# Edge convolution on a graph: Fori loops written out, index loads and key preparation batched by 13 chunks

## The chip, the cores and the metric

One core of one Trainium2 chip runs the kernel. The time is that of the device in microseconds for one launch. The kernel before was run three times: median 5047.05 us, lowest 5042.66, highest 5049.33. One further execution was taken with the hardware profiler; its rows are what this document reads.

## The reference

The graph has 12,500 nodes with 64 features and 400,000 edges, sorted by destination. Cut to what matters:

```python
h = relu(layernorm(x))
x_i, x_j = h[dst], h[src]
feat = concat([x_i, x_j - x_i], -1)                 # 128 values per edge
m = relu(feat @ W1 + b1) @ W2 + b2                  # 64 values per edge
out = segment_max(m, dst, num_segments=12500)       # 0 where a node has no edge
return x + where(isneginf(out), 0, out)
```

The first product splits in two tables of one row per node: a row a that belongs to the destination and a row b that belongs to the source. Per edge only relu(a[dst] + b[src]) @ W2 and a running maximum over the edges of one destination are left.

## The kernel before, in words

The 400,000 edges lie in 128 lanes of 3125 consecutive edges. A tile is one edge of every lane (128 x 64 values), a chunk is 12 tiles, and there are 260 chunks and a tail of 5 tiles. `rows` is a ring of 26 chunks. The prologue makes both tables, stores them to HBM, scatters the a rows to the places of the first edges of each node (`a_edges`) and turns the whole b table into bf16 pages in SBUF (`shared`). Then five engines run the chunks side by side, each with its own program order, held together by semaphores only. What each does for chunk c:

- POOL (GpSimd) waits until PE has turned chunk c-26, whose ring slot it takes (`z_turned`), and for the source indices (`src_loaded`), adds one to `chunk_open`, and gathers 11 tiles of b rows by 11 indirect DMAs (`gather_chunk`, L393; the loop is L432 to L439).
- The 12th tile is not gathered but picked on PE out of the bf16 pages. Its source index is split into an octet number and a place in the octet by two DVE instructions (`split_src`, L920 and L921, chunk c+5), converted to floats by ACT (L537), spread as a diagonal by ACT (`spread_keys`, L540), turned by PE (`turn_keys`, L666), compared with the page keys by DVE (`match_keys`, L935, chunk c+4), multiplied with the pages by PE (`pick`, L676, 37 matmuls for chunk c+3, 21 before the messages and 16 after them), masked by ACT (L549, chunk c+2), where `mark_octets` (L927) gave the mask, and summed by DVE (`choose`, L944).
- SP loads the a rows of the chunk into one of two halves of `a_fill` (`load_a`, L334, when `a_free` allows it) and, per chunk, the 12 columns of source indices for the chunk 26 ahead (L343).
- ACT scales the flags of a chunk (`flags`, L530 and L531, three chunks ahead), takes the relu of the turned sums (L560), and starts the store of the finished maxima (L567).
- DVE adds a and b rows (`add`, L897, chunk c+1), carries a rows along the lane where an edge does not start a node (`fill`, L885, chunk c+2, twelve dependent steps) and takes the running maximum (`maximum`, L911, chunk c, twelve dependent steps); fills and maxima alternate.
- PE turns the sums of the chunk (L687, 6 transposes), picks the first half for chunk c+3, makes the messages with W2 (L696, 12 matmuls), turns the keys of chunk c+5 and picks the second half.

The order on each engine is written by hand. SP, POOL, ACT, PE and DVE each have a `Fori` over 10 (or 9) iterations with 26 chunks unrolled in it, so semaphore targets and DMA addresses that depend on the iteration are computed in registers. At the loop's end three extra picks and five extra key turns are done for chunks that do not exist, with credits given on semaphores so that every iteration has the same counts.

After the last chunk a small epilogue carries maxima across lanes, gathers the maximum of every node (L456) and adds x.

Of the kernel before, what the change touches and what calls it, by code (L numbers as in the profile page):

```python
# [15 lines left out]
P = 128  # L16


def edge_conv(nc, x, src, dst, W1, b1, W2, b2, out):
# [25 lines left out]
    KEEP = RING // 2  # L45
# [16 lines left out]
    FILL_AHEAD = 3  # L62
    PAGES_FIRST = PAGES // 2 + 1

    with ExitStack() as ctx:
# [20 lines left out]
        src_idx = sb("src_idx", [P, RING, CHUNK], I32)  # L86
        same = sb("same", [P, TILES + (FILL_AHEAD + 1) * CHUNK])
        keep = sb("keep", [P, KEEP, 2, CHUNK])
# [60 lines left out]
        key_bits = sb("key_bits", [P, 2, 2], I32)  # L149
        key_octet = sb("key_octet", [P, 2, 2])  # L150
# [60 lines left out]
        src_first = sem("src_first")  # L211
        chunk_open = sem("chunk_open")
        src_loaded = [sem(f"src_loaded{s}") for s in range(RING // 2)]
        gathered = [sem(f"gathered{s}") for s in range(RING)]
        a_loaded = [sem(f"a_loaded{s}") for s in range(AE_RING)]
        a_free = sem("a_free")
# [29 lines left out]
        bits_split = sem("bits_split")  # L246
        bits_converted = sem("bits_converted")
# [28 lines left out]
        def _(sp):  # L276
            sp.dma_start(dst_rows[0:NP, :], dst.rearrange("(p k) -> p k", p=NP)).then_inc(samples_loaded, 16)
            for q in range(PIECES):
                sp.dma_start(xs[0:NP, q * PJ:(q + 1) * PJ, :],
                             x_nodes[:, q * PJ:(q + 1) * PJ, :]).then_inc(x_loaded[q], 16)  # L280
            sp.dma_start(src_idx[:, :, :].rearrange("p r k -> p (r k)"),
                         src_lanes[:, 0:RING * CHUNK]).then_inc(src_first, 16)
# [40 lines left out]
            for k in range(RING // 2):  # L323
                sp.sem_inc(src_loaded[k], 32)
# [5 lines left out]
            sp.wait_ge(bits_split, KEYS_AHEAD)  # L330

            def load_a(c, k, tiles=CHUNK):
                sp.wait_ge(a_free, c + 1)
                sp.dma_start(a_fill[:, k % AE_RING, 0:tiles * C],  # L334
                             a_lanes[:, bass.ds(c * W, tiles * C)]).then_inc(a_loaded[k % AE_RING], 16)

            with sp.Fori(0, ITERS - 1) as i:
                for k in range(RING):
                    load_a(i * RING + k, k)


                    sp.wait_ge(gathered[k], (i + 1) * 16 * GATHERED)
                    sp.dma_start(src_idx[:, k, :], src_lanes[:, bass.ds((i * RING + RING + k) * CHUNK, CHUNK)]  # L343
                                 ).then_inc(src_loaded[k // 2], 16)
            for k in range(RING):
                load_a((ITERS - 1) * RING + k, k)
                if k == 0:
                    sp.wait_ge(gathered[0], ITERS * 16 * GATHERED)
                    sp.dma_start(src_idx[:, 0, 0:TAIL], src_lanes[:, CHUNKS * CHUNK:TILES]
                                 ).then_inc(src_loaded[0], 16)  # L350


                    sp.sem_inc(src_loaded[0], 16)
                    for ahead in range(1, -(-KEYS_AHEAD // 2)):
                        sp.sem_inc(src_loaded[ahead], 32)
            load_a(CHUNKS, RING, TAIL)
            sp.sem_inc(a_loaded[(CHUNKS + 1) % AE_RING], 16)
            sp.wait_ge(picked, CHUNKS + PICK_AHEAD + FREE)
# [10 lines left out]
        def _(pool):  # L369
# [21 lines left out]
            def gather_chunk(slot, tiles=GATHERED, done=None):  # L391
                for t in range(tiles):
                    nc.gpsimd.indirect_dma_start(  # L393
                        out=rows[:, slot, t * C:(t + 1) * C], out_offset=None,
                        in_=b_table, in_offset=at(src_idx[:, slot, :], t)).then_inc(done or gathered[slot], 16)
# [11 lines left out]
            pool.wait_ge(src_first, 16)  # L407
# [24 lines left out]
            with pool.Fori(1, ITERS) as i:  # L432
                for k in range(RING):
# [6 lines left out]
            pool.wait_ge(z_turned, (CHUNKS - RING + 1) * GROUPS)  # L440
            pool.wait_ge(src_loaded[0], (ITERS + 1) * 32)
            gather_chunk(0, TAIL, ends_gathered)


            pool.wait_ge(state_stored[0], 16 * (CHUNKS // 2 + 2))
            pool.wait_ge(state_stored[1], 16 * (CHUNKS // 2 + 1))
# [15 lines left out]
        def _(act):  # L462
# [64 lines left out]
            def flags(c, k, tiles=CHUNK):  # L527

                now = same[:, bass.ds(c * CHUNK, CHUNK)]
                nc.scalar.activation(keep[:, k % KEEP, 0, :], now, ACT.Relu)  # L530
                nc.scalar.activation(keep[:, k % KEEP, 1, :], now, ACT.Copy, scale=FLT_MAX).then_inc(keep_ready, 1)  # L531

            def spread_keys(c, k):

                act.wait_ge(bits_split, c + 1)
                act.wait_ge(octets_marked, c - 1 + FREE)
                nc.scalar.activation(key_octet[:, k % 2, :], key_bits[:, k % 2, :], ACT.Copy).then_inc(bits_converted, 1)  # L537
                act.wait_ge(bits_converted, c + 1)
                act.wait_ge(keys_turned, c - 1 + FREE)
                nc.scalar.activation(key_diag[:, k % 2, :], ident_h[:, :], ACT.Copy,  # L540
                                     scale=key_octet[:, k % 2, 0:1]).then_inc(keys_spread, 1)
# [492 lines left out]
```

## Time and profile before

| | before |
|---|---|
| median of 3 runs (lowest to highest), us | 5047.05 (5042.66 to 5049.33) |
| profiled execution, own time / span, us | 5046.15 / 5044.3 |
| mean granted clock of TensorE, share of full | 0.794 |
| busy: PE, PE weight load | 3240.3 us (64%), 1876.2 us (37%) |
| busy: DVE, ACT, POOL | 2493.6 us (49%), 1025.4 us (20%), 3109.6 us (62%) |
| DMA packets, moved, mean rate | 239614, 452.86 MB, 90 GB/s |

The span is that of the profiled execution on the core. "Busy" leaves out register, branch, semaphore and DMA-issuing instructions. A granted clock of 1.0 is TensorE at 2.4 GHz, 0.5 is 1.2 GHz. A releaser called "remote" in a list of waits is one that the profile can't name, and "issue" is time in which an engine waited for nothing that is shown.

### The profile page before, as it was taken

To read this page: it belongs to the slowest core of one execution; us is meant where nothing else is said; L and a number is where in the kernel's file an instruction comes from. 1 tells how busy PE (TensorE), PEld (TensorE's weight loads), DVE (VectorE), ACT (ScalarE), POOL (GpSimd) and SP (SyncE) were. 2 spreads that over 40 slices of the span, in tenths; PEclk is the share of its full clock that TensorE was granted. 3 is DMA by queue.
4 is the path that set the end of the run, shared out by engine and by line. 5 is a ranking of instruction groups with operands and counts; after the bars stand their busy time and mean duration, and the time that the engine had idled before them with its cause. 6 is when DMAs were issued, how large, how long until landed. Compare 5 with 4: busy or idle time off the path is not lost.

```text
span 5044.3 us, 58734 instructions
## 1 busy us (share of the span) xinstructions
PE 3240.3 (64%) x14598; PEld 1876.2 (37%) x14861; DVE 2493.6 (49%) x8363; ACT 1025.4 (20%) x4057; POOL 3109.6 (62%) x3186
## 2 busy tenths in 40 slices
PE   2100137777777777777777777777777777777970
PEld 2100014444444444444444444444444444444540
DVE  4100115555555555555555555555555555556871
ACT  4300212212122121221212222122221212212320
POOL 5777756666666666666666666666666666664017
PEclk8555558888888888888888888888888888888985
DMA  7866312222222222222222222222222222222222
GB/s 274 315 229 227 115 32 73 67 73 70 70 73 67 73 70 70 70 70 73 70 70 69 70 73 69 70 70 69 73 67 73 70 70 72 69 72 71 80 77 56
DMA packets 239614, 452.86 MB, mean 90 GB/s; under 512 B 94781, under 2 KB 95402, under 8 KB 238738
## 3 DMA queue, kind: packets, MB, share of 16 engines
q1 hardware_dynamic: 97663, 225.75, 14.2%
q0 software_dynamic: 103216, 117.29, 11.1%
q10 hardware_dynamic: 38362, 105.62, 5.4%
q8 instruction: 140, 2.29, 0.2%
q14 instruction: 233, 1.91, 0.1%
HBM read 230.84 MB, written 217.71 MB: 89 GB/s over the span
## 4 chain that ended last, share of the span: by engine, by line
another core or an unknown queue 41%; issue 28%; DVE 10%; ACT 9%; PE 7%; POOL 2%; ACTq 2%; DMA 1%; DVEq 1%; POOLq 0%; SPq 0%
ACT dst_all L549 5%; DVE state L911 4%; PE ps_g L676 4%; DVE a_fill L885 3%; PE ps_m L696 2%; POOL a_rows L456 2%; ACT zt L560 2%; ACTq L567 1%; DMA shared<-in_x_dram 1%; DVE rows L897 1%; ACT zt L474 1%; ACT keep L531 1%; PE ps_t L687 0%; ACT shared L501 0%
## 5 line engine op out<-in xcount | busy, mean ns | idle before, releaser
L393 POOL DMA_INDIRECT rows<-b_table,src_idx x2865 | 2785.5, 972 | 1523.6 <-issue 805.7
L676 PE MATMUL ps_g<-shared,dst_all 128*128 128x512 bf16 x9468 | 2318.6, 400 | 174.3 <-issue 170.5
L676 PEld LDWEIGHTS ps_g<-shared,dst_all 128*128 128x128 bf16 x9731 | 1011.1, 105 | 1329.5 <-issue 417.3
L696 PE MATMUL ps_m<-w_diag,zt 128*128 128x128 f32 x3126 | 707.8, 411 | 920.2 <-ACT zt L560 917.8
L696 PEld LDWEIGHTS ps_m<-w_diag,zt 128*128 128x128 f32 x3126 | 638.2, 308 | 1056.3 <-ACT zt L560 1049.8
L911 DVE SCALAR_TENSOR_TENSOR state<-state,keep,ps_m 128x64 f32<-128x64 f32 x3125 | 862.3, 276 | 202.5 <-PE ps_m L696 166.7
L885 DVE SCALAR_TENSOR_TENSOR a_fill<-a_fill,keep 128x64 f32<-128x64 f32 x3144 | 879.6, 280 | 53.1 <-DVE a_fill L885 41.6
L935 DVE TENSOR_TENSOR dst_all<-ps_s,page_keys 128x1664 bf16<-128x1664 f32 x132 | 249.6, 1891 | 816.0 <-remote 795.1
L935 DVE TENSOR_TENSOR dst_all<-ps_x,page_keys 128x1664 bf16<-128x1664 f32 x132 | 249.6, 1891 | 794.7 <-remote 774.7
L560 ACT ACTIVATE zt<-ps_t 128x512 f32<-128x512 f32 (+1 forms) x521 | 226.4, 486 | 1517.9 <-remote 1511.6
L549 ACT ACTIVATE dst_all<-ps_g,dst_all 128x64 f32<-128x64 f32 x2096 | 458.1, 347 | 33.2 <-DVE rows L944 33.2
L530 ACT ACTIVATE keep<-same 128x12 f32 (+1 forms) x263 | 55.9, 213 | 1662.2 <-issue 929.0
L666 PE MATMUL ps_s<-dst_all,ones_h 128*128 128x128 f16 x133 | 40.2, 302 | 442.4 <-ACT dst_all L540 440.9
L897 DVE TENSOR_TENSOR rows<-rows,a_fill 128x512 f32<-128x512 f32 (+1 forms) x522 | 269.1, 557 | 33.2 <-issue 33.2
L944 DVE TENSOR_REDUCE rows<-dst_all 128x64 f32<-128x512 f32 x262 | 267.9, 1023 | 0.0
L687 PE MATMUL ps_t<-ident,rows 128*128 128x128 f32 x1563 | 213.5, 273 | 1.4 <-issue 1.4
L853 DVE TENSOR_TENSOR a_fill<-a_fill,shared 128x512 f32<-128x512 f32 x26 | 18.0, 693 | 383.3 <-issue 372.3
L687 PEld LDWEIGHTS ps_t<-ident,rows 128*128 128x128 f32 x1563 | 186.8, 141 | 53.0 <-issue 3.5
L666 PEld LDWEIGHTS ps_s<-dst_all,ones_h 128*128 128x128 f16 x133 | 19.2, 145 | 442.8 <-issue 440.0
L447 POOL DMA_INDIRECT head<-states,lane_i x1 | 0.9, 942 | 261.2 <-DMA states<-state 261.2
L401 POOL DMA_INDIRECT rows<-in_dst_dram,blk_idx x101 | 102.6, 1016 | 73.5 <-issue 24.4
L419 POOL DMA_INDIRECT a_edges<-a_rows,first_idx x100 | 108.8, 1088 | 31.3 <-issue 31.3
(116 smaller groups left out, 877.0 us busy)
## 6 DMA issues: line engine op xcount, KB each, us to landing
a_edges<-state SPq DMA_DIRECT2D x80, 1250.0 KB
a_fill<-a_edges SPq DMA_DIRECT2D x260, 384.0 KB
states<-state ACTq DMA_DIRECT2D x260, 384.0 KB
rows<-b_table,src_idx POOLq DMA_INDIRECT x2865
src_idx<-in_src_dram SPq DMA_DIRECT2D x234, 6.0 KB
shared<-in_x_dram SPq DMA_DIRECT2D x5, 625.0 KB
b_table<-shared ACTq DMA_DIRECT2D x5, 625.0 KB
a_table<-a_rows SPq DMA_DIRECT2D x1, 3125.0 KB
```

The lines of the kernel that those rows point to most:

```text
L393: nc.gpsimd.indirect_dma_start(out=rows[:, slot, t * C:(t + 1) * C], out_offset=None, in_=b_table, in_offset=at(src_idx[:, slot, :], t)).t ...
L419: nc.gpsimd.indirect_dma_start(out=a_edges, out_offset=at(first_idx, j), in_=a_rows[:, j, :], in_offset=None, bounds_check=E - 1, oob_is_e ...
L549: last = nc.scalar.activation(masked[:, o, :], ps_g[:, k % 2, o * C:(o + 1) * C], ACT.Copy, scale=octet_is[:, k % RING, o:o + 1])
L560: last = nc.scalar.activation(zt[:, g, 0:full], ps_t[:, g, 0:full], ACT.Relu)
L676: last = nc.tensor.matmul(ps_g[:, half, :], key_is[:, half, g, :], table[:, g, t, :], start=(g, t) == (0, 0), stop=g == PAGES - 1)
L687: last = nc.tensor.transpose(ps_t[0:m * C, g, a * C:a * C + P], rows[:, k, t * C:(t + m) * C], ident[:, :])
L696: last = nc.tensor.matmul(ps_m[:, g, a * C:(a + m) * C], zt[0:m * C, g, a * C:a * C + P], w2_pair[0:m * C, 0:m * C], start=True, stop=True)
L885: nc.vector.scalar_tensor_tensor(here, before, keep[:, k % KEEP, 0, t:t + 1], here, ALU.mult, ALU.add).then_inc(fill_step, 1)
L897: nc.vector.tensor_tensor(rows[:, k, part], rows[:, k, part], a_fill[:, k % AE_RING, part], ALU.add).then_inc(z_ready, 1)
L911: nc.vector.scalar_tensor_tensor(state[:, half, t * C:(t + 1) * C], before, keep[:, k % KEEP, 1, t:t + 1], ps_m[:, g, r * C:(r + 1) * C], ...
L935: nc.vector.tensor_tensor(key_is[:, half, :, :], ps_k[half].rearrange("p (o e) -> p o e", o=1).to_broadcast((P, PAGES, P)), page_keys[:, : ...
L944: nc.vector.tensor_reduce(rows[:, k, W - C:W], masked[:, :, :].rearrange("p o c -> p c o"), AX_X, ALU.add).then_inc(chosen, 1)
```

## The change

All `Fori` loops over chunks are written out, so that semaphore targets and addresses are constants. The source indices get a ring of three batches of 13 chunks; a batch is one DMA, issued in the middle of the earlier one. POOL waits for it only at a batch's first chunk, and `chunk_open` goes. DVE splits the picked source indices of 13 chunks at once, converts them itself and marks their octets with one instruction. ACT makes the flags of 13 chunks at once, four chunks ahead. SP's load of the a rows waits for the first fill of the chunk before (`fill_step`) where it waited for the credit `a_free`. Picks, masks, key turns and fills for chunks behind the last one are left out, and with them the credits on the stores. The diff's core, with "..." where lines are left out:

```diff
-    KEEP = RING // 2
-    FILL_AHEAD = 3
+    BATCHED = 13
+    BATCHES = -(-(CHUNKS + 1) // BATCHED)
+    SRC_RING = 3
+    SPLIT_AHEAD, FLAGS_AHEAD = KEYS_AHEAD + 2, 4
...
-        src_idx = sb("src_idx", [P, RING, CHUNK], I32)
-        keep = sb("keep", [P, KEEP, 2, CHUNK])
+        src_idx = sb("src_idx", [P, SRC_RING, BATCHED, CHUNK], I32)
+        keep = sb("keep", [P, 2, 2, BATCHED * CHUNK])
...
 SP
-            with sp.Fori(0, ITERS - 1) as i:
-                for k in range(RING):
-                    load_a(i * RING + k, k)
-                    sp.wait_ge(gathered[k], (i + 1) * 16 * GATHERED)
-                    sp.dma_start(src_idx[:, k, :], src_lanes[:, bass.ds((i * RING + RING + k) * CHUNK, CHUNK)]
-                                 ).then_inc(src_loaded[k // 2], 16)
...
+            for c in range(CHUNKS + 1):
+                if c % BATCHED == 1 and SRC_RING <= c // BATCHED + 2 < BATCHES:
+                    q = c // BATCHED + 2
+                    over = (q - SRC_RING) * BATCHED + BATCHED - 1
+                    sp.wait_ge(gathered[over % RING], (over // RING + 1) * 16 * GATHERED)
+                    sp.wait_ge(keys_split, q - SRC_RING + 1)
+                    load_src(q)
+                tiles = CHUNK if c < CHUNKS else TAIL
+                if c >= 1:
+                    sp.wait_ge(fill_step, (c - 1) * CHUNK + 1)
+                sp.dma_start(a_fill[:, c % AE_RING, 0:tiles * C],
+                             a_lanes[:, c * W:c * W + tiles * C]).then_inc(a_loaded[c % AE_RING], 16)
...
 POOL
+                q, j = divmod(c, BATCHED)
+                if j == 0:
+                    pool.wait_ge(src_loaded[q % SRC_RING], (q // SRC_RING + 1) * 16)
...
-            with pool.Fori(1, ITERS) as i:
-                for k in range(RING):
-                    pool.wait_ge(z_turned, (i * RING + k - RING + 1) * GROUPS)
-                    pool.wait_ge(src_loaded[k // 2], (i + 1) * 32)
-                    pool.sem_inc(chunk_open, 1)
-                    gather_chunk(k)
+            for c in range(RING, CHUNKS + 1):
+                pool.wait_ge(z_turned, (c - RING + 1) * GROUPS)
+                if c < CHUNKS:
+                    gather_chunk(c)
+                else:
+                    gather_chunk(c, TAIL, ends_gathered)
...
 ACT
-            def flags(c, k, tiles=CHUNK):
-                now = same[:, bass.ds(c * CHUNK, CHUNK)]
+            def flags(q):
+                tiles = min(BATCHED * CHUNK, TILES - q * BATCHED * CHUNK)
+                now = same[:, q * BATCHED * CHUNK:q * BATCHED * CHUNK + tiles]
...
-                act.wait_ge(bits_split, c + 1)
-                act.wait_ge(octets_marked, c - 1 + FREE)
-                nc.scalar.activation(key_octet[:, k % 2, :], key_bits[:, k % 2, :], ACT.Copy).then_inc(bits_converted, 1)
-                act.wait_ge(bits_converted, c + 1)
+                act.wait_ge(keys_split, q + 1)
...
-                if tiles == CHUNK:
-                    flags(c + FILL_AHEAD, k + FILL_AHEAD)
+                if (c + FLAGS_AHEAD) % BATCHED == 0 and c >= BATCHED - FLAGS_AHEAD:
+                    flags((c + FLAGS_AHEAD) // BATCHED)
+                if c + KEYS_AHEAD < CHUNKS:
                     spread_keys(c + KEYS_AHEAD, k + KEYS_AHEAD)
...
 PE
-                if whole:
+                if c + PICK_AHEAD < CHUNKS:
                     pick(c + PICK_AHEAD, k + PICK_AHEAD, range(PAGES_FIRST))
...
 DVE
-                if t == 1:
-                    dve.sem_inc(a_free, 1)
...
+            def split_keys(q):
+                half = q % 2
+                column = src_idx[:, q % SRC_RING, :, CHUNK - 1]
+                dve.wait_ge(src_loaded[q % SRC_RING], (q // SRC_RING + 1) * 16)
+                link(nc.vector.tensor_scalar(key_bits[:, 0, :], column, 3, None, ALU.logical_shift_right))
+                link(nc.vector.tensor_scalar(key_bits[:, 1, :], column, OCTET - 1, None, ALU.bitwise_and))
+                if q >= 2:
+                    dve.wait_ge(keys_spread, (q - 1) * BATCHED + FREE)
+                nc.vector.tensor_copy(key_octet[:, half, :, :], key_bits[:, :, :]).then_inc(keys_split, 1)
+                dve.wait_ge(keys_split, q + 1)
+                if q >= 2:
+                    dve.wait_ge(octet_masked, (q - 1) * BATCHED + FREE)
+                nc.vector.tensor_tensor(
+                    octet_is[:, half * BATCHED:(half + 1) * BATCHED, :],
+                    octets[:, :].rearrange("p (k o) -> p k o", k=1).to_broadcast((P, BATCHED, OCTET)),
+                    key_octet[:, half, 1, :].rearrange("p (k o) -> p k o", o=1).to_broadcast((P, BATCHED, OCTET)),
+                    ALU.is_equal).then_inc(octets_marked, 1)
...
+            for c in range(CHUNKS):
+                add(c + 1)
+                if (c + SPLIT_AHEAD) % BATCHED == 0 and c + SPLIT_AHEAD < CHUNKS:
+                    split_keys((c + SPLIT_AHEAD) // BATCHED)
+                if c + MATCH_AHEAD < CHUNKS:
+                    match_keys(c + MATCH_AHEAD)
+                filled = tiles_of(c + 2) if c + 2 <= CHUNKS else 0
+                if filled:
+                    fill_ready(c + 2)
+                if c >= 2:
+                    dve.wait_ge(state_stored[c % 2], c // 2 * 16)
```

## Rows read from the trace of the kernel before

**Rows 1.** The page: first line and its rows of the instruction queues (packets, MB, share).

```profile
span 5044.3 us, 58734 instructions
...
q8 instruction: 140, 2.29, 0.2%
q14 instruction: 233, 1.91, 0.1%
```

**Rows 2.** Waits in 1000 to 4600 us: engine, line, releaser, total us, times, longest us.

```profile
ACT zt L560 <- remote: 1409.8, 217, 7.4
DVE dst_all L935 <- remote: 1348.7, 211, 8.1
...
POOL rows L393 <- issue: 660.5, 2167, 0.3
POOL rows L393 <- remote: 629.0, 217, 3.3
```

**Rows 3.** Timeline of one chunk: start, us, engine, line, operation, [idle before <-releaser].

```profile
3007.13 0.82 PE L687 MATMUL ps_t<-ident,rows 128*128 128x128 f32 x6
...
3008.03 0.20 ACT L537 ACTIVATE key_octet<-key_bits 128x2 f32<-128x2 int32 x1 [0.17 <-issue]
...
3015.32 0.87 ACT L560 ACTIVATE zt<-ps_t 128x512 f32<-128x512 f32 x2 [6.65 <-remote]
...
3015.97 2.93 PE L696 MATMUL ps_m<-w_diag,zt 128*128 128x128 f32 x12 [3.48 <-ACT zt L560]
...
3016.14 0.94 POOL L393 DMA_INDIRECT rows<-b_table,src_idx  x1 [2.80 <-remote]
...
3031.91 0.87 ACT L560 ACTIVATE zt<-ps_t 128x512 f32<-128x512 f32 x2 [6.61 <-remote]
```

**Rows 4.** Timeline of two bursts of gathers and the relus behind them.

```profile
1138.36 0.94 POOL L393 DMA_INDIRECT rows<-b_table,src_idx  x1 [2.84 <-remote]
...
1151.43 0.94 POOL L393 DMA_INDIRECT rows<-b_table,src_idx  x1 [0.30 <-issue]
...
1154.13 0.87 ACT L560 ACTIVATE zt<-ps_t 128x512 f32<-128x512 f32 x2 [6.44 <-remote]
...
1154.95 0.94 POOL L393 DMA_INDIRECT rows<-b_table,src_idx  x1 [2.58 <-remote]
...
1167.43 0.94 POOL L393 DMA_INDIRECT rows<-b_table,src_idx  x1 [0.30 <-issue]
...
1170.71 0.87 ACT L560 ACTIVATE zt<-ps_t 128x512 f32<-128x512 f32 x2 [2.12 <-remote]
```

**Rows 5.** Stretches: length, busy us (count) of the engines, PEclk, DMA share, GB/s.

```profile
2998.70:3015.30 16.60, 12.93 (x55) 7.39 (x56) 9.04 (x31) 3.41 (x14) 10.79 (x11) 0.80 0.26 71
4698.80:4708.90 10.10, 10.05 (x57) 5.80 (x57) 9.10 (x32) 3.36 (x16) 0.00 (x0) 1.00 0.24 80
...
626.00:704.00 78.00, 16.15 (x30) 2.98 (x29) 2.15 (x4) 2.23 (x10) 59.97 (x55) 0.52 0.10 28
704.00:726.00 22.00, 5.55 (x10) 1.08 (x11) 0.00 (x0) 0.00 (x0) 0.00 (x0) 0.50 0.01 1
```

**Rows 6.** DMA in 2000 to 3000 us: all packets; queue, packets, MB, share.

```profile
DMA packets 47161, 70.28 MB, mean 70 GB/s; under 512 B 21136, under 2 KB 21136, under 8 KB 47072
...
q1 hardware_dynamic: 17280, 23.97, 9.1%
```

**Rows 7.** Timeline of ACT: first steady relu, and the relu at the steady stage's end.

```profile
756.49 0.85 ACT L560 ACTIVATE zt<-ps_t 128x512 f32<-128x512 f32 x2
...
4627.05 0.87 ACT L560 ACTIVATE zt<-ps_t 128x512 f32<-128x512 f32 x2 [1.87 <-remote]
```

**Rows 8.** Timeline: POOL's scatter of the head, whose only wait is for DVE.

```profile
4897.04 0.22 DVE L1001 TENSOR_TENSOR head_new<-head,ps_s 128x64 f32<-128x64 f32 x1 [3.38 <-DMA head<-states,lane_i]
4897.54 0.99 POOL L450 DMA_INDIRECT states<-head_new,lane_i  x1 [2.08 <-DVE head_new L1001]
```

More of the change, by code:

```diff
@@ L588, in _ @@
             act.wait_ge(same_ready, 1)
-            for c in range(FILL_AHEAD):
-                flags(c, c)
-            for half in range(2):
-                act.sem_inc(state_stored[half], 16)
+            flags(0)
             act.sem_inc(octet_masked, FREE)
@@ L681, in step @@
             def step(c, k, tiles=CHUNK):
-                whole = tiles == CHUNK
                 for g, n in groups(tiles):
@@ L710, in _ @@
                     pick(c + PICK_AHEAD, c + PICK_AHEAD, range(PAGES))
-            with pe.Fori(0, ITERS) as i:
-                for k in range(RING):
-                    step(i * RING + k, k)
-            step(CHUNKS, 0, TAIL)
+            for c in range(CHUNKS):
+                step(c, c)
+            step(CHUNKS, CHUNKS, TAIL)
             pe.wait_ge(max_step, CHUNKS * CHUNK + TAIL + 1)
@@ L877, in fill, with fill_ready @@
+            def fill_ready(c):
+                dve.wait_ge(a_loaded[c % AE_RING], (c // AE_RING + 1) * 16)
+                dve.wait_ge(keep_ready, c // BATCHED + 1)
+            def fill(c, t):
+                slot = c % AE_RING
                 if t == 0:
-                    before = a_fill[:, (slot - 1) % AE_RING, W - C:W]
+                    before = a_fill[:, 1 - slot, W - C:W]
                 else:
                     before = a_fill[:, slot, (t - 1) * C:t * C]
+                if c * CHUNK + t > 0:
@@ L896, in add @@
                     part = slice(g * GROUP * C, (g * GROUP + n) * C)
-                    nc.vector.tensor_tensor(rows[:, k, part], rows[:, k, part], a_fill[:, k % AE_RING, part],
-                                            ALU.add).then_inc(z_ready, 1)
-            def maximum(c, k, t):
-                half = k % 2
+                    nc.vector.tensor_tensor(rows[:, c % RING, part], rows[:, c % RING, part],
+                                            a_fill[:, c % AE_RING, part], ALU.add).then_inc(z_ready, 1)
@@ L903, in maximum @@
+            def maximum(c, t):
+                half = c % 2
                 g, r = divmod(t, GROUP)
@@ L933, in match_keys @@
+            def match_keys(c):
+                half = c % 2
                 dve.wait_ge(keys_turned, c + 1 + FREE)
@@ L957, in _ @@
-            for c in range(-KEYS_AHEAD, 0):
-                prepare_picks(c, c, 0, match=c >= -MATCH_AHEAD)
+            split_keys(0)
+            for c in range(MATCH_AHEAD):
+                match_keys(c)
             LEAD = 2
             def fill_all(c):
-                fill_ready(c, c, 0)
+                fill_ready(c)
                 for t in range(CHUNK):
-                    fill(c, c, t)
-            choose(0, 0)
+                    fill(c, t)
+            choose(0)
             fill_all(0)
-            add(0, 0, 0, 0)
@@ L989, in _ @@
-            dve.wait_ge(state_stored[0], (ITERS * (RING // 2) + 1) * 16)
+            for c in range(CHUNKS):
+                add(c + 1)
[8 more added lines that the diff above has]
+                    dve.wait_ge(state_stored[c % 2], c // 2 * 16)
+                for t in range(CHUNK + LEAD):
+                    if t == CHUNK - 2 and c + CHOOSE_AHEAD < CHUNKS:
+                        choose(c + CHOOSE_AHEAD)
+                    if t < filled:
+                        fill(c + 2, t)
+                    if t >= LEAD:
+                        maximum(c, t - LEAD)
```

171 lines of the change are left out of this document (57 added, 114 removed).

## The prediction

> **What bounds the kernel now.** I went from the page's busy shares to the wait lists of the steady stage, then to the timeline of one chunk, then to a chunk of the stage without gathers. No engine is full: the page has PE at 64% and POOL at 62% of 5044.3 us [rows 1]. The first steady relu of ACT starts at 756.49 and the one that ends the stage at 4627.05 [rows 7]; 234 gathered chunks in about 3871 us are 16.6 us a chunk. The wait lists say that ACT (1409.8 us) and DVE (1348.7 us) both wait, 6.5 us a chunk, for a releaser that the profile can't name, and so does POOL, 2.9 us a chunk [rows 2].
>
> The timeline of one chunk names it [rows 3]. PE's transposes start at 3007.13 and have run by 3008. ACT's relu (L560) waits for them alone and starts at 3015.32, over 7 us later; DVE's match_keys, which waits for PE too, loses 6.4 us a time (1348.7 / 211) [rows 2]; POOL, which needs a transposes' signal for its ring slot, issues at 3016.14. The next relu is at 3031.91, 16.59 later. So PE's signals are late while POOL's gathers run. Without gathers they are not: a chunk of the drain takes 10.10 us, PE busy for 10.05 of it [rows 5].
>
> Is it the end of POOL's burst that lets them through? No [rows 4]. One burst goes from 1138.36 to 1151.43 (13.07 us between first and last start), the next from 1154.95 to 1167.43 (12.48); the relus follow at 1154.13 and 1170.71, each 15.8 us after the first gather. The wait is counted from where the burst starts and is indifferent to when it ends, as if a backlog had to drain. The prologue shows such a backlog: from 626 to 704 us PE starts 30 matmuls in 78 us although nothing it needs is missing, and from 704 to 726 still only 10 in 22 us, with ACT, DVE and POOL at 0 and DMA at 1 GB/s [rows 5]. My reading: PE's signals and starts share some path with what gathers and other transfers leave on it, and the drain of that path sets the 16.6 us.
>
> The Trainium skill (NOTIFIC — the notification-queue block, section 7.1 Overflow) says that the block that takes the engines' and DMAs' records can hold a producer back when it fills, rather than lose records. The trace neither names the block nor contradicts it; by that rule fewer instructions and packets mean earlier signals, which is my forecast.
>
> **The change part by part.** The profiled execution took 5046.15 us, 1.85 more than its span and 0.9 below the median of the runs; the sums are against it.
>
> *Source indices in batches.* 234 loads of 128 x 48 B become 18 of 128 x 624 B. In 1000 us (60 chunks) q1 has 17280 packets, 288 a chunk; in all there are 47161, 786 a chunk [rows 6]. A q1 chunk holds one a_fill load and one src_idx load, so I put half, 144, to src_idx; batched it is about 11 a chunk. Some 133 of 786 packets go. SP itself isn't late. The batch's load waits for the gathers of a batch done long before; it is issued 25 chunks ahead of need or so and no one waits for it.
>
> *POOL's waits.* Each chunk now waits for z_turned, then src_loaded, then adds to chunk_open, then gathers: 0.82 us from the common release (3015.32) to the gather (3016.14) [rows 3]. After the change 216 of 234 chunks have one wait, which can sit on the gather itself. The nearest row is POOL L450, which has only that: DVE L1001 ends at 4897.26, L450 starts at 4897.54, 0.28 later [rows 8]. The saving is 0 to 0.54 us a chunk; I take 0.54, the row with the same form: 216 x 0.54 = 117 us, if the burst's start is in the cycle, as rows 4 say.
>
> *Flags, splitting, conversion, octet marks.* Per chunk ACT loses L530, L531 and L537 (0.2 us each [rows 3]), DVE two shifts and the L927 mark (about 0.5 us together, by ACT's rows of like size). They stand just before the waits of over 6 us, which hide them now. If that cover goes, DVE's chunk is 9.04 us of work in 16.6 and ACT's 3.41 [rows 5], so they still hide. Once in 13 chunks come about six instructions of 0.2 to 0.4 us, bounded by nothing and by 13 x 0.6 us; hidden too, value 0. Skipping the shifts moves the rest of DVE's chunk at most 0.3 us earlier.
>
> *Loops written out.* Register, branch and address instructions go. What it might cost is fetching the code: instruction queues moved 2.29 + 1.91 MB for 58734 instructions, 71 B each, so the loops' code already comes in once per execution and not once per program [rows 1]. Zero, bounds -5 to +5 us. The Trainium skill (Runtime: NRT & Kernel Launch, Instruction fetch mechanics) has a taken branch stall the fetch; ten such stalls per engine would be gained by it, but they would fall into the waits above.
>
> *Credits and the ends.* SP's a_fill load waits for the first fill of the next chunk instead of a credit given after it: same moment. PE skips the picks of the last three chunks; PE's 10.1 us a chunk then falls to DVE's 9.1 less its match and reduce (2.9), but signals between the engines remain: about 7, so 3 x 3 = 9 us saved. The other end work (order of the prologue's matches, one flags pair for 13 chunks) lies before the crawl up to 726 us and is put at 0, bounds -5 to +5.
>
> *Sum.* Of the load per chunk, 786 packets and about 217 instructions of all kinds (58734 in the whole program, most of them in 261 chunks), some 133 packets and, by my count of the diff, 44 instructions go (the 6 named, an issue and waits of SP, two waits of POOL, and the register and address ones): 177 of 1003, 18%. If the 15.8 us from first gather to release shrinks with it, it becomes 13.0, plus 0.28 for the wait: 13.3. That is shorter than POOL's own burst: gathers follow each other by 1.248 (12.48 / 10), 11 of them take 13.7, and DVE's add stretches them by up to 0.6 (13.07 against 12.48) [rows 4], so 14.2 with some of it. POOL then becomes the bound. PE, busy 12.93 at a granted clock of 0.80 [rows 5], still fits. 234 x (16.6 - 14.2) = 562, with the 9 of the end 571: 5046 - 571 = 4475, **4470 us**. The drain of 25 chunks at 10 us stays if the ring's lead stays; if signals come early enough that the compute side keeps its 13.3 or less, it eats the lead (234 x (14.2 / 13.3 - 1) = 16 chunks, all 25 at 12.8) and 160 to 250 us more go: 4220. At the other end half the relief gives a period near 15.2: 5046 - 328 - 9 = about 4710. Own range 4220 to 4710.
>
> **The rivals.**
> *Only the burst's start moves.* The delay after the first gather is a constant of the gathers, not of the load: src_idx packets are 48 B and few, and PE's own instructions, which do not change, may be what queues. For it: 15.8 in both bursts of rows 4. Then only POOL's 0.54 is saved: 5046 - 117 - 9 = 4920 us.
>
> *Nothing in the steady stage.* The release is counted from the previous release or from PE's own work, so an earlier burst brings nothing, and all the batched work was hidden: 5046 - 9 = 5037 us, on the edge of what can be told from no change (0.2%, 10 us). For it: each removed instruction stands beside a wait of over 6 us. Against: in rows 4 two bursts of different length kept the distance from the first gather.
>
> *Slower.* The signals of PE's messages (L696, from 3015.97 on) must come through while POOL begins its burst. Today the burst starts at 3016.14, and the messages run until about 3018.9, the first group of 8 tiles until about 3018 [rows 3], between the second and third gather. With the burst 0.54 earlier a third gather is out when this first signal is due; if that holds it, it is held as long as the transposes' signal, 7.3 us, and DVE's maxima, next add and the next transposes all shift by that, nothing else in the cycle being slack. It decides from the point where the messages' signal comes behind the third gather of its burst. With every fifth chunk hit: 234 / 5 x 7.3 = 342, 5046 + 342 - 9 = about 5380 us; a few chunks only would cancel the gain. Against it: the burst's start varies little today and no chunk of the steady stage is so hit.
>
> **How the numbers follow.** The lighter path, with POOL as the bound: 42%. Only the burst's start: 22%. Nothing in the steady stage: 19%. Slower: 17%. The forecast is the first one's, 4470. The range goes from 4220, its low end, through the second to the third rival's 5037: 4220 to 5040, which leaves out the slower case and little else. Faster by over 0.2% take the first two and over half of the third, 0.74; within 0.2% the rest of the third and a slower case that just cancels, 0.10; slower 0.16.
>
> **What would show it.** Right: relus in the steady stage 14.2 us apart, ACT's unnamed wait at about 4 us a chunk or less, POOL waiting for "issue" only, q1 with some 155 packets a chunk, POOL's first gather 0.3 us after the release. If the distance from first gather to relu is still 15.8 with fewer packets, the load reading is wrong and the second case holds; if the gather comes 0.3 after the release and the period is still 16.6, the third does. Maxima that start 7 us or more after the messages are the slower case. The prediction is wrong as a whole if the granted clock or PE's busy time per chunk, and not the signals' delay, is what changes.

## The result and the profile after

The changed kernel takes 4905.19 us (median of 4 runs, 4903.07 to 4908.01), the kernel before 5044.85 beside it: a ratio of 0.9725, 95% interval 0.971 to 0.9739, or 140 us. Its profiled execution has a span of 4906.2 us, against 5044.3. The forecast was 4470; the time is that of the second case, 4920.

| | before | after |
|---|---|---|
| instructions, DMA packets | 58734, 239614 | 47353, 208533 |
| mean granted clock of TensorE | 0.794 | 0.799 |
| first relu of ACT, us | 743.7 | 738.6 |
| POOL's last steady gather, us | 4632.3 | 4503.3 |
| from there to the end, us | 412.0 | 402.9 |

The prologue gives 5.1 us, the end 9.1, and what lies between 123.9, or 0.53 us in each of 234 chunks.

The wait list of the steady stage after, 1000 to 4400 us (engine, line, releaser, total, times, longest), answers to [rows 2]:

```profile
ACT zt L547 <- remote: 1499.4, 211, 7.9
DVE dst_all L924 <- remote: 1461.9, 211, 7.2
...
POOL rows L386 <- issue: 645.2, 2117, 0.3
POOL rows L386 <- remote: 551.6, 211, 2.7
```

ACT waits 7.1 us a chunk for PE's signal where it waited 6.5: the work taken from ACT came back as waiting, and PE's signals are as late as ever. Only POOL's wait got shorter, 2.9 to 2.6. The timeline of one chunk says where, beside [rows 3]:

```profile
3011.69 0.82 PE L669 MATMUL ps_t<-ident,rows 128*128 128x128 f32 x6
...
3016.20 0.94 POOL L386 DMA_INDIRECT rows<-b_table,src_idx  x1 [0.30 <-issue]
...
3019.45 0.87 ACT L547 ACTIVATE zt<-ps_t 128x512 f32<-128x512 f32 x2 [7.07 <-remote]
...
3019.73 0.94 POOL L386 DMA_INDIRECT rows<-b_table,src_idx  x1 [2.58 <-remote]
...
3020.10 2.93 PE L678 MATMUL ps_m<-w_diag,zt 128*128 128x128 f32 x12 [3.06 <-ACT zt L547]
...
3035.46 0.87 ACT L547 ACTIVATE zt<-ps_t 128x512 f32<-128x512 f32 x2 [7.05 <-remote]
```

Relu to first gather is 0.28 us (was 0.82), first gather to next relu 15.73 (was 15.77): the first moved by what was predicted, the second not at all.

If something piles up behind the gathers, it is not their transfers. In the chunk above, the packets of queue q0, which carries the gathers' rows, in the windows 3005.19 to 3006.50 and 3017.70 to 3019.00 are those of the burst's first and of its last gather; behind them, from 3018.60 to the relu, engines and DMA are all at 0:

```profile
q0 software_dynamic: 32, 0.03, 12.1%
...
q0 software_dynamic: 32, 0.03, 13.9%
```

```profile
3018.60:3019.45 0.85, 0.00 (x0) 0.00 (x0) 0.00 (x0) 0.00 (x0) 0.00 (x0) 1.00 0.00 0
```

Over 210 chunks the first packet of the first gather and that of the last both start 1.65 us behind their gather (medians), and the last gather's last packet has ended 1.2 us before the relu.

Engines and transfers of the same chunk and of the crawl in the prologue, and the packets of 1000 us, beside [rows 5, 6]:

```profile
3003.42:3019.45 16.03, 12.75 (x55) 7.35 (x56) 8.85 (x28) 2.91 (x11) 10.40 (x11) 0.81 0.28 73
626.00:704.00 78.00, 15.78 (x27) 2.90 (x28) 1.89 (x1) 1.74 (x8) 58.58 (x55) 0.50 0.09 28
704.00:726.00 22.00, 5.52 (x11) 1.05 (x10) 0.00 (x0) 0.00 (x0) 0.00 (x0) 0.50 0.00 0
```

```profile
DMA packets 40697, 72.74 MB, mean 73 GB/s; under 512 B 13040, under 2 KB 13680, under 8 KB 40640
...
q1 hardware_dynamic: 9648, 24.78, 9.0%
```

Packets a chunk are 654 (786 before), DVE and ACT have 6 instructions fewer in the chunk's window. The load did fall by what was reckoned; the delay didn't follow it.

### The profile page after: what moved, and what is told of

Read it like the earlier page. It is cut to its first block, busy times and chain, and to the rows that moved or that the text cites. A ratio compares the mean times of both kernels' runs of the same rounds, so it can differ in the third digit from the quotient of the medians.

```text
span 4906.2 us, 47353 instructions
## 1 busy us (share of the span) xinstructions
PE 3227.3 (66%) x14485; PEld 1841.1 (38%) x14745; DVE 2427.4 (49%) x7621; ACT 893.1 (18%) x3287; POOL 3047.4 (62%) x3186
## 2 busy tenths in 40 slices
DMA packets 208533, 451.67 MB, mean 92 GB/s; under 512 B 61389, under 2 KB 64442, under 8 KB 207778
## 4 chain that ended last, share of the span: by engine, by line
another core or an unknown queue 41%; issue 28%; DVE 11%; ACT 9%; PE 6%; POOL 2%; DMA 1%; ACTq 1%; DVEq 0%; POOLq 0%; SPq 0%
ACT dst_all L535 5%; PE ps_g L659 5%; DVE state L896 4%; DVE a_fill L869 4%; POOL a_rows L443 2%; DVE rows L882 2%; ACT zt L547 1%; ACT dst_all L526 1%; ACTq L554 1%; DMA shared<-in_x_dram 1%; PE ps_m L678 1%; ACT zt L461 1%; ACT shared L568 0%; ACT shared L488 0%
## 5 line engine op out<-in xcount | busy, mean ns | idle before, releaser
L386 POOL DMA_INDIRECT rows<-b_table,src_idx x2865 | 2724.1, 951 | 1456.8 <-issue 804.3
L678 PE MATMUL ps_m<-w_diag,zt 128*128 128x128 f32 x3126 | 681.0, 399 | 726.0 <-ACT zt L547 722.5
L678 PEld LDWEIGHTS ps_m<-w_diag,zt 128*128 128x128 f32 x3126 | 611.1, 296 | 901.1 <-ACT zt L547 893.3
L535 ACT ACTIVATE dst_all<-ps_g,dst_all 128x64 f32<-128x64 f32 x2080 | 454.7, 347 | 123.9 <-remote 80.5
L526 ACT ACTIVATE dst_all<-ident_h,key_octet 128x128 f16<-128x128 f16 x260 | 104.1, 401 | 1449.5 <-issue 1236.0
```

Source lines behind the costliest of these rows:

```text
L386: nc.gpsimd.indirect_dma_start(out=rows[:, c % RING, t * C:(t + 1) * C], out_offset=None, in_=b_table, in_offset=at(src_idx[:, q % SRC_RIN ...
L535: last = nc.scalar.activation(masked[:, o, :], ps_g[:, k % 2, o * C:(o + 1) * C], ACT.Copy, scale=octet_is[:, k % RING, o:o + 1])
L678: last = nc.tensor.matmul(ps_m[:, g, a * C:(a + m) * C], zt[0:m * C, g, a * C:a * C + P], w2_pair[0:m * C, 0:m * C], start=True, stop=True)
```

## The experiments

Theory A: between relu and relu lie a stretch from relu to POOL's first gather, which the change shortens by 0.54 us, and a fixed 15.8 us that the gathers alone set. Rival B: the lighter load pays. For each kernel the trace gives the two stretches, as medians over some 210 chunks (spread 0.1 us). They were run on five chips, here numbered 1 to 5, and on each chip the kernel before was run beside them. This turned out to matter. Times of e2, e3, e4, e5, e10, e12, e13 and e16 are of one execution each:

| chip | before, us | kernel | relu to first gather | first gather to relu | period | time, us |
|---|---|---|---|---|---|---|
| (that of the prediction) | 5045 | before | 0.82 | 15.80 | 16.61 | 5045 |
| | | changed | 0.28 | 15.79 | 16.07 | 4905 |
| 1 | 5048 | e1_waits_back | irregular | irregular | 16.8 | 5090 |
| 1 | | e2_small_loads | 0.28 | 15.81 | 16.09 | 4911 |
| 1 | | e3_nine_gathers | 0.28 | 13.01 | 13.29 | 4261 |
| 1 | | e4_spaced2 | 0.28 | 15.89 | 16.17 | 4939 |
| 2 | 4109 | e6, e7, e3_ten, e5 | POOL never waits | | 13.8, 13.9 (e6, e7) | 4107, 4102, 3797, 4328 |
| 3 | 4080 | e8, e9, e10, e11 | POOL never waits | | 13.9 (e8) | 4079, 4080, 4337, 4077 |
| 4 | 5048 | e12, e13 | by stretch, below | | | 4961, 5041 |
| 5 | 5052 | e14_before_one_wait | 0.28 | 15.95 | 16.24 | 4957 |
| 5 | | e15 (changed) | 0.28 | 15.80 | 16.08 | 4910 |
| 5 | | e16_ten_gathers | 0.28 | 14.41 | 14.69 | 4582 |

**Undoing POOL's waits.**

```diff
-                if j == 0:
+                if j == 0 or c >= RING:
                     pool.wait_ge(src_loaded[q % SRC_RING], (q // SRC_RING + 1) * 16)
+                if c >= RING:
+                    pool.sem_inc(chunk_open, 1)
```

> The changed kernel with one part undone: POOL again waits for src_loaded in every chunk and adds one to a semaphore before it gathers; all else stays batched. Theory A (the gain is POOL's earlier burst alone, since relu follows the burst's first gather by 15.8 us whatever else is done): the first gather comes 0.82 us after the relu again, the period is 16.6 us, the time 4905 + 234 x 0.54 = 5031 us. Rival B (part of the gain is the lighter load of packets and instructions, which stay light here): the distance from first gather to relu stays shorter than before's and the time stays at or under 4960 us.

5090.24 us, ratio 1.0091 to before (1.0074 to 1.0108): the gain is lost and 42 us more. Both theories missed: the direction is theory A's, the 5031 us aren't, and the stretches are irregular. Its waits in 1000 to 4600 us:

```profile
ACT dst_all L529 <- DVE state L899: 1509.2, 129, 29.0
DVE state L899 <- remote: 1089.6, 74, 22.9
```

DVE's maxima now wait up to 22.9 us for the signal of the messages, which neither kernel has in its list; the longest wait of a maximum for the messages is 4.7 us in the kernel before. That is the slower case of the prediction, found not in the change but in this neighbour of it: a messages' signal that comes too late in a burst is held with the others. The kernel before has the same waits at the same place and stays regular; why the changed kernel doesn't is not shown.

**Giving the small packets back.**

```diff
+                if c < CHUNKS:
+                    if c >= 1:
+                        sp.wait_ge(spare_loaded, 16 * c)
+                    sp.dma_start(spare[:, :], src_lanes[:, c * CHUNK:(c + 1) * CHUNK]).then_inc(spare_loaded, 16)
```

> The changed kernel with a load of 128 x 48 B from HBM to an unused tile added on SP in every chunk, so that the packets per chunk are those of before again, and POOL's waits are not. Theory A: the period stays at 16.07 us, the distance from first gather to relu at 15.8. Rival B (load on a shared path): the distance grows, by up to a sixth.

Packets in 1000 us are up by a fifth from the 40697 of the changed kernel, and the period moves by 0.02 us. As a load of packets rival B falls.

```profile
DMA packets 49594, 73.11 MB, mean 73 GB/s; under 512 B 21952, under 2 KB 22592, under 8 KB 49536
```

**Fewer gathers.** The gather loop runs over 9 tiles (e3) or 10 (e16) in place of 11, with the counts of `gathered` to match; the rows of the tiles left out stay stale.

> The changed kernel with two of the eleven gathers of each chunk left out from chunk 26 on (their rows stay stale, so this part of the computation is left out). Theory A1 (each gather holds something for 1.435 us, 11 of them 15.79): first gather to relu becomes 9 x 1.435 = 12.9 us. Theory A2 (the last gather's start plus 3.3 us): 8 x 1.249 + 3.3 = 13.3 us. Rival C (a fixed 15.8 us, a matter of PE or of time, not of the gathers): 15.8 stays. Under A1 and A2 PE's 13.0 us of work per chunk at these clocks is close to being the bound, so the period is 13.2 to 13.6.

> The changed kernel with ten gathers a chunk (one tile's rows stay stale, so this part of the computation is left out). On a chip where before takes 5048: first gather to relu 14.40 us if gathers drain at 1.39 us each (15.79 with 11, 13.01 with 9), 14.54 if the release is counted from the last gather. On the other kind of chip POOL's own 12.6 us a chunk.

13.01, 14.41 and 15.80 us for 9, 10 and 11: 1.40 and 1.39 us a gather, though gathers start 1.25 us apart. For ten, a drain of 1.39 us a gather had forecast 14.40 and a release counted from the last gather 14.54. With ten gathers (e16), the last gather of a burst, the relu behind it, the first gather of the next burst and the relu behind that:

```profile
3008.93 0.94 POOL L386 DMA_INDIRECT rows<-b_table,src_idx  x1 [0.31 <-issue]
...
3012.14 0.87 ACT L547 ACTIVATE zt<-ps_t 128x512 f32<-128x512 f32 x2 [5.77 <-remote]
...
3012.42 0.94 POOL L386 DMA_INDIRECT rows<-b_table,src_idx  x1 [2.54 <-remote]
...
3026.78 0.87 ACT L547 ACTIVATE zt<-ps_t 128x512 f32<-128x512 f32 x2 [5.72 <-remote]
```

The relu comes 3.1 us behind the last gather's start in the median, with nine 3.0, with eleven 3.3. It is as if each gather, issued every 1.25 us, left something that takes 1.39 us to drain, and PE's signals were held until all of it had gone. The linear growth is measured; the drain is a reading of it, and what drains is not the gathers' packets, which keep pace with POOL. The growth with the number of gathers alone is why burst length had no say in [rows 4]: 11 x 1.39 + 0.5 us is the same whether POOL issues them in 12.5 or 13.1 us.

**Spacing by semaphores.** Two `sem_inc` behind each gather.

> The changed kernel with two semaphore increments on POOL behind every gather, so that gathers start some 1.5 to 1.8 us apart and not 1.25. Theory A1 (each gather holds a path for 1.435 us and PE's signals pass only when it is empty): with gathers further apart than that the path empties between two of them, PE's signals arrive within about 1.5 us of their matmuls, ACT's unnamed wait of 7 us goes, and POOL's burst of 11 spacings becomes the period. Theory A2 (signals pass behind the last gather of a burst): relu follows the last gather by 3.3 us again, period 10 spacings + 3.6 us. Rival C: relu 15.8 us after the first gather or with the burst's end, whichever is later.

They did not space anything: gathers stay 1.25 us apart, so this tests no theory. The increments don't slow POOL down, yet the period is 0.1 us longer and the time 28 us above e2's on the same chip. The trace has PE itself held late in the bursts: in 1000 to 3800 us its picks wait 579 us for "issue", against 114 in the changed kernel and 61 before. So instructions other than gathers are not without any effect on PE; how they act is open.

**The other chips.** On chip 2 the kernel before takes 4109 us, on chip 3 4080.

> The kernel before with one part of the change alone: POOL's loop written out, chunk_open gone, and the wait for src_loaded put ahead of the wait for z_turned, so that the last wait before the first gather is the one for PE. Per-chunk loads of indices, flags, splits and all loops of the other engines stay. Theory A: relu to first gather falls from 0.82 to 0.28 us, the period from 16.61 to 16.07, the time to 5047 - 127 = 4920 us, which is nearly the whole gain. Rival B (batching and fewer instructions matter): less than half of the gain, above 4980 us.

> The changed kernel with the same wait for src_loaded and the same semaphore increment in every chunk as in e1_waits_back, but ahead of the wait for z_turned. Theory A (only what POOL does between PE's signal and the first gather counts): as the changed kernel, 4905 us, first gather 0.28 us after the relu. Rival (the instructions as such disturb POOL or the order): slower, near the 5090 us of e1_waits_back.

> The changed kernel with one of the eleven gathers of each chunk left out from chunk 26 on (its rows stay stale, so this part of the computation is left out). First gather to relu was 15.79 us with 11 and 13.01 with 9, 1.39 a gather. Theory A1 (a queue served at 1.39 us a gather): 14.40 us with 10. Theory A2 (last gather's start plus a constant 3.3): 11.24 + 3.3 = 14.54.

> The changed kernel with a memset of an unused tile on POOL behind every gather, which waits for the memset before: 1 column up to chunk 99, 128 columns from 100 to 179, 256 columns from 180 on. Gathers should start 1.35 to 1.7 us apart. Theory A1 (PE's signals are held once gathers have piled up, and the pile drains at 1.39 us a gather): where the spacing is below 1.39 nothing changes, relu stays 15.8 us after the first gather; where it is above, nothing piles up, PE's signals arrive at once, ACT's unnamed wait of 7 us goes and the period becomes 11 spacings with no pause between the bursts. Rival C (signals are held through any burst, whatever its pace): relu follows the last gather by about 3 us at every spacing, the period grows by 10 times what a gather is delayed.

> The changed kernel itself, beside the kernel before, on the chip that this call gets. In the last call the kernel before took 4109 us and not 5048, with POOL's gathers back to back and PE's signals arriving at once, so chips differ. Theory D (the hold-up of PE's signals behind piled-up gathers belongs to some chips): on a chip where before takes 5048 the changed kernel takes 4905 again; on one where before takes 4109, POOL's gathers bound both and the changed kernel is within 0.5% of it. Rival (the change helps by the same 127 us on every chip): 3980 us there.

> The kernel before with POOL's loop written out, without chunk_open, and with the wait for PE last, as in e6_before_one_wait. On a chip where before takes 5048: theory A 4920 us, first gather 0.28 us after the relu and period 16.07; rival B above 4980. On a chip where before takes 4109: no difference, as measured.

> The changed kernel with a memset behind each gather, 1 column up to chunk 99, 128 columns to chunk 179, 256 columns after: spacings 1.25, 1.33 and 1.44 us, as measured on the other chip. On a chip where before takes 5048: theory A1 (gathers drain at 1.39 us each and PE's signals are held when they have piled up) has periods near 16.1 at the first two spacings and, at 1.44, signals at once, no pause between bursts and a period of 15.8 with the ring's lead used up; rival C (any burst holds signals) has 16.1, 16.9 and 18.0. On the other kind of chip as before, 4328 us.

> The changed kernel with per-chunk src_loaded wait and increment ahead of the wait for PE, as in e7_waits_before. On a chip where before takes 5048: theory A 4905 us and 0.28 us from relu to gather; rival near the 5090 of e1_waits_back. On the other kind of chip no difference.

On these two chips no engine waits for an unnamed releaser in 1000 to 3600 us, and no matmul of the picks waits over 0.3 us for "issue": PE's signals are not held. So none of these runs can tell theory A from rival B. (e6 and e9 also had the flaw that e13 shows below.) A stretch of the changed kernel (e8), and its window 626 to 704 us, in which [rows 5] has 30 matmuls:

```profile
1208.26 0.82 PE L669 MATMUL ps_t<-ident,rows 128*128 128x128 f32 x6
...
1209.38 0.94 POOL L386 DMA_INDIRECT rows<-b_table,src_idx  x1 [0.31 <-issue]
...
1210.61 0.85 ACT L547 ACTIVATE zt<-ps_t 128x512 f32<-128x512 f32 x2
1210.62 0.97 POOL L386 DMA_INDIRECT rows<-b_table,src_idx  x1 [0.30 <-issue]
```

```profile
626.00:704.00 78.00, 49.41 (x269) 28.70 (x270) 48.57 (x152) 19.54 (x56) 59.13 (x62) 0.79 0.31 87
```

269 matmuls stand where 30 stood, relus follow without a wait, chunks take 10.0 us until the ring's lead of 25 chunks is used up, and then POOL's back-to-back gathers set the pace. The chain that ended last in e8 is POOL's for 57% of the span. There the change is worth nothing: e8 has the ratio 0.9997 (0.9987 to 1.0007), e9 0.9998, e11 0.9997, e6 0.9996, e7 0.9979 (0.9969 to 0.9989). With the fillers the gathers start 1.25, 1.33 and 1.44 us apart in the three stretches, and the times are 4328 and 4337 us.

**Stretches in one trace.** e12, on chip 4, changes POOL's work along the run. The waits of e1 are set behind the wait for PE or ahead of it; the filler is

```diff
+                    if c >= 175 and done is None:
+                        if fillers[0]:
+                            pool.wait_ge(filled_up, fillers[0])
+                        nc.gpsimd.memset(spare[:, 0:128 if c < 210 else 256], 0.0).then_inc(filled_up, 1)
+                        fillers[0] += 1
```

> The changed kernel with five stretches of chunks that differ in what POOL does, to be read one by one in the trace: chunks 26 to 69 and 110 to 124 as changed; 70 to 109 per-chunk wait for src_loaded and increment ahead of the wait for PE; 125 to 174 the same two behind it, as before had them; 175 to 209 a memset of 128 columns behind each gather (spacing 1.33 us), 210 to 259 one of 256 columns (1.44 us). On a chip where before takes 5048: theory A1 has periods 16.07, 16.07 (first gather 0.28 us after the relu), then 16.6 or irregular with 0.82, then 16.1 at spacing 1.33, and at 1.44 PE's signals at once, no pause between bursts and 15.8. Rival C (any burst holds signals till it has ended) has 16.9 and 18.0 in the last two. On a chip where before takes 4100 PE's signals are never late and the stretches differ by POOL's own pace alone: 13.8, 13.8, 13.8, 14.7, 15.8.

| chunks | POOL | relu to first gather | gather spacing | POOL's period |
|---|---|---|---|---|
| 27 to 69 | as changed | 0.28 | 1.25 | 16.08 |
| 70 to 109 | wait and increment ahead | 0.28 | 1.25 | 16.09 |
| 110 to 124 | as changed | 0.28 | 1.25 | 16.08 |
| 125 to 174 | wait and increment behind | 0.82 in the median, -4.9 to 5.7 | 1.25 | 16.8, spread 2.3 |
| 175 to 209 | filler, 128 columns | 0.28 in the median, -5.5 to 3.4 | 1.34 | 16.4 |
| 210 to 259 | filler, 256 columns | (no pause) | 1.44 | 16.25 |

Here the relu is that of the chunk whose ring slot POOL takes, and a negative stretch is a relu that comes behind the gather. The same two instructions cost nothing ahead of the wait for PE and upset the order behind it. The fillers decide for neither A1 nor C: with 128 columns the period is 16.4, where A1 had 16.1 and C 16.9, with 256 it is 16.25, where A1 had 15.8 and C 18.0. By A1 nothing should pile up at 1.44 us a gather. POOL doesn't pause any more, yet PE now crawls, as in the prologue, a pair of matmuls with each gather:

```profile
4302.20 0.95 POOL L393 DMA_INDIRECT rows<-b_table,src_idx  x1 [0.17 <-issue]
4302.54 0.59 PE L675 MATMUL ps_g<-shared,dst_all 128*128 128x512 bf16 x2 [0.88 <-issue]
...
4304.06 1.89 DVE L940 TENSOR_TENSOR dst_all<-ps_s,page_keys 128x1664 bf16<-128x1664 f32 x1 [3.27 <-remote]
...
4305.44 0.87 ACT L563 ACTIVATE zt<-ps_t 128x512 f32<-128x512 f32 x2 [4.72 <-remote]
```

So at 1.44 us a gather PE gets on a little, and the picture of a pile that has to be empty doesn't hold as it stands. There is no faster version in it: the period is above 16.08, and the ring's lead is hardly used.

**The kernel before with POOL's order alone.**

> The kernel before with POOL's loop written out: chunks 26 to 139 with the waits and the increment in the order of before, 140 to 259 with the wait for src_loaded first, the wait for PE last and no increment; all other parts as before. On a chip where before takes 5048: theory A has a period of 16.6 us with 0.82 from relu to gather in the first half and 16.07 with 0.28 in the second, rival B (batched work and fewer packets are needed for it) 16.4 or more in the second. On a chip where before takes 4100 both halves are at POOL's own 13.8.

Periods of 16.62 and 16.58, 0.82 and 0.76 us from relu to gather. The first half shows that writing POOL's loop out is worth nothing. The second is a miss: in the trace the wait for PE is still an instruction of its own and the gather carries the other wait. The next one puts the increment between them:

```diff
-            with pool.Fori(1, ITERS) as i:
+            for i in range(1, ITERS):
                 for k in range(RING):
-                    pool.wait_ge(z_turned, (i * RING + k - RING + 1) * GROUPS)
                     pool.wait_ge(src_loaded[k // 2], (i + 1) * 32)
                     pool.sem_inc(chunk_open, 1)
+                    pool.wait_ge(z_turned, (i * RING + k - RING + 1) * GROUPS)
```

> The kernel before with POOL's loop written out and its three steps in another order: wait for src_loaded, increment chunk_open (which takes that wait with it), wait for PE, gather. In e13_before_halves the wait for PE had come out as an instruction of its own ahead of a gather that carried the other wait, and 0.76 us were left; here the gather carries the wait for PE. On a chip where before takes 5048: theory A has 0.28 us from relu to first gather, period 16.07, time 4920 us; rival B (batching needed) 5030 us or more. On a chip where before takes 4100: no difference.

> The changed kernel beside the kernel before on this chip. On a chip where before takes 5048: 4905 us, and e14 within 20 us above it, which is what the rest of the change (last three picks and prologue) is worth. On a chip where before takes 4100: no difference.

e14 takes 4956.68 us, ratio 0.9812 (0.9795 to 0.9828); the changed kernel 4909.82, ratio 0.972 (0.9704 to 0.9736). The timeline of e14:

```profile
3012.73 0.87 ACT L558 ACTIVATE zt<-ps_t 128x512 f32<-128x512 f32 x2 [0.34 <-remote]
...
3013.01 0.94 POOL L393 DMA_INDIRECT rows<-b_table,src_idx  x1 [2.51 <-remote]
...
3028.95 0.87 ACT L558 ACTIVATE zt<-ps_t 128x512 f32<-128x512 f32 x2 [2.42 <-remote]
```

So the place of one wait makes 95 of 142 us. e14's 4957 us lie between theory A's 4920 and rival B's 5030, nearer to A, and 47 us above the changed kernel, where at most 20 had been expected. Of the 47 left, by the two traces, 4 lie before the first relu, 10 behind the last gather and 33 in the steady stage, where e14's first gather to relu is 15.95 and not 15.80. The trace of e14 shows what comes with these 0.15 us: as in e4, PE's picks are held late in the burst (620 us of "issue" in 1000 to 3800), the messages start 3.2 us behind the relu in the median and not 0.65, and ACT's unnamed wait is 2.9 us a time where the changed kernel has 7.1. A pick held in e14, with the next one 1.44 us behind it:

```profile
3025.87 0.38 PE L674 MATMUL ps_g<-shared,dst_all 128*128 128x512 bf16 x1 [0.94 <-issue]
...
3027.31 0.38 PE L674 MATMUL ps_g<-shared,dst_all 128*128 128x512 bf16 x1 [1.06 <-issue]
```

Which of the batched parts removes this is open; the packets given back in e2 cost 0.02 us.

## Why the prediction was wrong, step by step

- *The period is the stretch to the first gather plus a constant, and burst length has no part in it*: right; all 210 chunks have it. *PE's signals are late and come together*: right.
- *POOL's wait on the gather saves 0.54 us*: right, 0.82 to 0.28. All 234 gathered chunks have the short form, those at a batch's start too, and not 216: 0.53 x 234 = 124 us for 117. e14 puts the order alone at 95, as 0.15 us of the 0.54 are given back while the rest of the kernel is as before.
- *If the 15.8 us shrink with the load*: this step failed, and the forecast with it. The load fell by 132 packets and 44 instructions a chunk, the 15.8 stayed, and e2 gave the packets back for 0.02 us. The constant is 1.39 us for each of 11 gathers plus 0.5. Two signs of it stood in the trace of before: the distance was equal in every chunk, and the scatters in the crawl of the prologue started 1.40 us apart, where the gathers of the steady stage start 1.25 apart and the scatters on chips 2 and 3 1.25 to 1.29. I took the content of the backlog for everything on the chip, where its length goes by the gathers. That other instructions weigh nothing is not shown: e4 and e14 have 15.89 and 15.95.
- The Trainium skill's rule of a record block that holds producers back (NOTIFIC — the notification-queue block, section 7.1 Overflow) would have made the delay fall with instructions and packets. Here 11381 instructions and 31081 packets fewer left it at 15.8; the measurement decides against that use of the rule, though no run shows what the held path is or whether records have a part in it.
- *Flags, splits, conversion hidden*: right, ACT's wait grew from 6.5 to 7.1 us a chunk by what was taken from its work. *Loops written out at zero*: POOL's alone was worth nothing (e13, first half); the other engines' loops were not run by themselves.
- *The batch's load is issued 25 chunks ahead of need*: wrong, it is issued 46 us, 2.9 chunks, before POOL's first gather that uses it. That no one waits for it was right.
- *The end*: 9 us reckoned, 9.1 measured. *Prologue at 0, bounds 5*: 5.1.
- *The slower case*: late messages' signals do occur (e1), but not in this change, and the third gather is not where it turns. The messages end 3.3 us after the first gather in the changed kernel and 5.4 us in e14's chunk, and their signals still pass; z_turned's, from 7.5 us on, are all held to 15.8.
- What no case had: that all this is a trait of some chips. Where signals come at once even the kernel before takes 4080 to 4109 us, below the 4220 that I put at the low end, and by the mechanism named there: POOL's own pace and a used-up lead.
- The time is within 15 us of the second case's 4920 (22%). That case had the constant as one of the gathers, which the runs bear out, beside a guess at PE's own instructions, which they don't.

## What to carry to other kernels

Where a group of DMA-issuing instructions starts off a fixed delay, look at what stands between the signal and the first of them: put every other wait and increment ahead of the wait that comes last, so that the first instruction carries that one alone. When a wait is constant to 0.1 us, count what it is a multiple of (leave out one and two of the repeated instructions) before taking it for a load. And compare only beside the old kernel on the same chip: the same two kernels differ by 2.8% on one chip and by nothing on another. Last, look in the trace at which instruction carries which wait: two waits written in an order needn't come out in it (e13), and an increment put between them kept them apart (e14).

## What the runs showed of the hardware

- Three chips of five hold PE's signals behind bursts of indirect gathers of 128 rows x 256 B; before takes 5048 to 5052 us there, 4080 and 4109 on the two others, 23% apart with the same program. The chip of the prediction (5045) is of the first kind; whether it is one of the three isn't on record.
- On the first kind the delay grows by 1.39 to 1.40 us a gather (three sizes), while POOL issues at 1.25 and the gathers' packets follow each by 1.65. DVE's signals pass at once meanwhile (in [rows 3]'s chunk ACT's store starts at 3007.08, 0.16 us behind the maximum that it waits for), and ACT's can: of 37 relus that start 5 to 12 us into a burst in e1, 16 have PE's messages 0.05 us behind their first half, the others later, by up to 4 us, where PE may have been busy. PE's matmul starts are held too, late in a burst (e4, e14) or throughout where POOL doesn't pause (e12's last stretch, the prologue's crawl).
- A wait carried by the gather costs 0.28 us from the signal, one on an instruction of its own ahead of it 0.76, with a second wait and an increment on that instruction 0.82. Two increments behind each gather left the spacing at 1.25 us; memsets of 128 and 256 columns make it 1.33 and 1.44.
